# Second attention of a four-layer block: projections cut in halves over all sixteen units, GpSimd's subtractions cut in quarters

## The reference, cut to what matters

```python
h  = rmsnorm(layernorm(x)) * ln_w            # 1024 tokens x 512
q  = h @ wq.T                                # 32 heads of 16
k, v = ctx @ wk.T, ctx @ wv.T                # 8 key/value heads, 64 context rows for each batch
p  = softmax(q @ k.T / 4)                    # for each head: 256 tokens x 64 context rows
x  = x + tanh(gate) * ((p @ v) @ wo.T)
```

## Time and profile before

| what | value |
|---|---|
| time, median of 3 runs | 1511.48 us (1511.46 to 1512.91) |
| the profiled execution | 1511.66 us |
| its span | 1509.9 us |
| PE busy over the span | 1348.9 us, 89% |
| DVE busy | 1121.3 us, 74% |
| ACT, POOL busy | 677.9 us, 336.3 us |
| units of the second attention | from 475.90 us (first `turn_p`) to 576.94 us (last `weigh`) |

### The profile page before, as it was taken

One profiled execution on the slowest core, in us unless ns is written; L12 is line 12 of the kernel. 1 busy time (PEld: TensorE's weight loads), 2 busy tenths in 40 slices (PEclk: granted clock), 3 DMA queues, 4 the chain that ended last, 5 costly groups with the idle time before them and its releaser, 6 DMA issues.

```text
span 1509.9 us, 18648 instructions
## 1 busy us (share of the span) xinstructions
PE 1348.9 (89%) x6492; PEld 970.2 (64%) x6492; DVE 1121.3 (74%) x2045; ACT 677.9 (45%) x1405; POOL 336.3 (22%) x380
## 2 busy tenths in 40 slices
PE   8999999999998989967999998999999999999104
PEld 5665666566575648736888875777777777778102
DVE  4788898888898986985555576666666566567998
ACT  4778777778423434432222224443434444443104
POOL 1112121211163020332111021312222212213620
PEclk9999999999999999988999998999999999999557
DMA  5677888789710011522211210101201101000001
GB/s 218 170 180 184 221 230 209 162 211 224 213 42 1 1 56 34 107 64 50 71 42 42 96 70 1 70 28 43 70 29 43 66 14 62 1 1 1 0 0 56
DMA packets 37910, 127.74 MB, mean 85 GB/s; under 512 B 4944, under 2 KB 10960, under 8 KB 31680
## 3 DMA queue, kind: packets, MB, share of 16 engines
q1 hardware_dynamic: 26304, 83.38, 16.0%
q0 software_dynamic: 11520, 43.26, 15.0%
HBM read 72.63 MB, written 10.75 MB: 55 GB/s over the span
## 4 chain that ended last, share of the span: by engine, by line
PE 58%; DVE 23%; ACT 6%; DVEq 6%; DMA 4%; issue 2%; POOL 1%; POOLq 1%; SPq 0%
PE PS L150 12%; PE PS L152 11%; PE PS L151 11%; DVE AR L676 4%; PE PS L925 4%; PE PS L963 4%; DMA AR<-AR 2%; ACT s_sb L606 2%; DVE AR L2598 2%; PE PS L949 2%; DVE AR L2587 2%; DVE AR L2594 2%; DVEq L666 1%; DVE AR L682 1%; PE PS L1537 1%
## 5 line engine op out<-in xcount | busy, mean ns | idle before, releaser
L438 POOL DMA_DIRECT2D AR<-AR x76 | 74.9, 1104 | 339.8 <-DMA AR<-AR 125.8
L151 PE MATMUL PS<-R16r 128*128 128x512 f32 (+1 forms) x328 | 122.8, 374 | 0.0
L535 PE MATMUL PS<-R,PT 128*128 128x512 f32 x256 | 116.1, 596 | 3.7 <-DVE X L716 3.7
L152 PE MATMUL PS<-R16r 128*128 128x512 f32 (+1 forms) x312 | 119.0, 382 | 0.0
L510 PE MATMUL PS<-R,HT 128*128 128x256 f32 x512 | 116.5, 381 | 2.1 <-ACT R L595 2.1
L510 PEld LDWEIGHTS PS<-R,HT 128*128 128x128 f32 x512 | 94.8, 190 | 15.2 <-ACT R L595 3.6
L1083 ACT COPY AR<-PS 128x512 f32<-128x512 f32 x64 | 37.5, 587 | 145.9 <-PE PS L152 145.5
L606 ACT ACTIVATE s_sb<-PS,sm 128x64 f32<-128x64 f32 x256 | 78.1, 335 | 52.4 <-DVE sm L701 52.0
L150 PE MATMUL PS<-HTr,R16r 128*128 128x512 f32 (+1 forms) x240 | 91.5, 381 | 3.0 <-DVE R16r L190 1.6
L150 PE MATMUL PS<-R16r,HTr 128*128 128x512 f32 (+1 forms) x224 | 90.2, 403 | 0.0
L152 PE MATMUL PS<-HTr,R16r 128*128 128x512 f32 (+1 forms) x240 | 88.3, 368 | 0.0
(11 more groups left out here) (313 smaller groups left out, 3513.6 us busy)
## 6 DMA issues: line engine op xcount, KB each, us to landing
AR<-AR POOLq DMA_DIRECT2D x76, 528.0 KB, 6.6
OR<-in_wo SPq DMA_DIRECT2D x12, 1024.0 KB, 12.4
dequantised<-AR SPq DMA_DIRECT2D x8, 1056.0 KB, 5.5
WR<-in_w0q SPq DMA_DIRECT2D x8, 1024.0 KB, 11.4
AR<-in_w3q SPq DMA_DIRECT2D x8, 1024.0 KB, 4.9
WR<-dequantised SPq DMA_DIRECT2D x22, 256.0 KB, 2.8
AR<-in_nf SPq DMA_DIRECT2D x4, 1056.0 KB, 9.4
nf_in<-in_nf SPq DMA_DIRECT2D x4, 1056.0 KB, 10.2
```

Source lines behind the costliest of these rows:

```text
L151: nc.tensor.matmul(out, ah, bl, start=False, stop=False)
L152: return nc.tensor.matmul(out, al, bh, start=False, stop=last_)
L438: nc.gpsimd.dma_start(nf_below(g)[:, part], what[:, part], accum_op=ALU.add, max_dma_last_dim=4 * N_NF // 2).then_inc(added, 16)
L535: i = nc.tensor.matmul(bank(5 + tt), PT[:, at:at + P], vo[:, pr, b, :], start=pr == 0, stop=pr == 1)
```

## The change

`project_q` and `project_o` take a tuple of halves and issue only those matmuls; the second half counts up the semaphore. A list, `projections(u)`, says which halves follow `turn_p(u)`: one half in most units, two in units 3, 6, 8 and 14, twenty in all from unit 0 to unit 15. `add` and `dve_stats` move: `add(0,0)` and `add(0,1)` to units 8 and 9, `add(1,0)` and `add(1,1)` to 11 and 13, `add(2,0)` to 15, `add(2,1)` with its statistics behind the loop. The copies of queries on ACT move to units 1, 3, 5 and 7. Both of GpSimd's subtractions are cut into four: of the first, pieces 1, 2 and 3 wait for `probs` of 1, 2 and 3; of the second, pieces 0 to 3 wait for `probs` of 11, 12, 13 and 14. The semaphores `o_split` and `F1["split"]` count with the last piece.

```diff
@@ pool_a1
-            pool_low(Oh[:], Ol[:], OR[:]).then_inc(A1["o_split"], 1)
+            for c in range(C):
+                cols = slice(c * D, (c + 1) * D)
+                if c:
+                    pool.wait_ge(A1["probs"], c)
+                i = pool_low(Oh[:, cols], Ol[:, cols], OR[:, cols])
+            i.then_inc(A1["o_split"], 1)
@@ pe_a1
-            def project_q(b, pr):
-                if b:
+            def project_q(b, pr, halves=(0, 1)):
+                if b and halves[0] == 0:
                     pe.wait_ge(A1["qT_ready"], 2 * b - 1 + pr)
-                if b >= 3 and pr == 1:
-                    pe.wait_ge(A1["acc"], 2 * b - 4)
-                for hh in range(2):
+                for hh in halves:
...
+            def projections(u):
+                if u < 2:
+                    project_q(2, 0, (u,))
+                elif u == 2:
+                    project_q(2, 1, (0,))
+                elif u == 3:
+                    project_q(2, 1, (1,))
+                    project_q(3, 0, (0,))
+                elif u == 4:
+                    project_q(3, 0, (1,))
+                elif u == 5:
+                    project_q(3, 1, (0,))
+                elif u == 6:
+                    project_q(3, 1, (1,))
+                    project_o(0, 0, (0,))
+                elif u == 7:
+                    project_o(0, 0, (1,))
+                elif u == 8:
+                    project_o(0, 1)
+                elif u < 13:
+                    project_o(1, (u - 9) // 2, ((u - 9) % 2,))
+                elif u == 13:
+                    project_o(2, 0, (0,))
+                elif u == 14:
+                    project_o(2, 0, (1,))
+                    project_o(2, 1, (0,))
                 else:
+                    project_o(2, 1, (1,))
@@
                 turn_p(u)
-                if at < 2 and b:
-                    project_o(b - 1, at)
-                if at > 1 and b + 2 < B:
-                    project_q(b + 2, at - 2)
+                projections(u)
@@ act_a1
-                if at > 1 and b + 2 < B:
-                    queries(b + 2, at - 2)
+                if u in (1, 3, 5, 7):
+                    queries(2 + u // 4, u // 2 % 2)
@@ dve_a1
-                if 0 < hc < 3 and b:
-                    add(b - 1, hc - 1)
-                    if hc == 2:
-                        dve_stats(dve, b - 1)
+                if u == 8:
+                    add(0, 0)
+                elif u == 9:
+                    add(0, 1)
+                    dve_stats(dve, 0)
+                elif u == 11:
+                    add(1, 0)
+                elif u == 13:
+                    add(1, 1)
+                    dve_stats(dve, 1)
+                elif u == 15:
+                    add(2, 0)
             norm_low(dve, 3, 0)
             norm_scaled(dve, 3, 2)
+            add(2, 1)
             norm_low(dve, 3, 1)
             norm_scaled(dve, 3, 3)
+            dve_stats(dve, 2)
@@ pool_f1
             pool.wait_ge(F1["w_hi"], 1)
-            pool_low(Wh[:, 0:C * NWF], Wl[:, 0:C * NWF], WR[:, 0:C * NWF]).then_inc(F1["split"], 1)
+            for c in range(C):
+                cols = slice(c * NWF, (c + 1) * NWF)
+                pool.wait_ge(A1["probs"], NU - 5 + c)
+                i = pool_low(Wh[:, cols], Wl[:, cols], WR[:, cols])
+            i.then_inc(F1["split"], 1)
             pool_norm(pool, 3)
```

More of the change, by code:

```diff
@@ L1525, in project_q @@
                                 HTl[:, c, tok], c == 0, c == C - 1)
-                i.then_inc(A1["q_mm"], 1)
+                if halves[-1]:
+                    i.then_inc(A1["q_mm"], 1)
             def scores(u):
@@ L1558, in weigh, with project_o @@
                 i.then_inc(A1["pv_mm"], 1)
[L1560 to L1564, removed]
-                else:
[L1566 to L1574, removed]
+            def project_o(b, tt, halves=(0, 1)):
+                if halves[0] == 0:
+                    if tt == 0:
+                        pe.wait_ge(A1["olo"], (b + 1) * C)
+                        if b == 0:
+                            pe.wait_ge(A1["o_split"], 1)
+                    else:
+                        pe.wait_ge(A1["qT_ready"], 2 * B)
+                    if b:
+                        pe.wait_ge(A1["acc"], 2 * b - 1 + tt)
+                hi, lo = out1(b)
+                for half in halves:
+                    for hc in (2 * half, 2 * half + 1):
+                        tok = slice(hc * S + tt * P, hc * S + tt * P + P)
+                        i = mm3(bank(0 if tt else 7), hi[:, tok], lo[:, tok], Oh[:, hc * D:(hc + 1) * D],
+                                Ol[:, hc * D:(hc + 1) * D], hc == 0, hc == C - 1)
+                if halves[-1]:
+                    i.then_inc(A1["wo_mm"], 1)
```

## The result

The changed kernel takes 1514.38 us in the median of 19 runs, the kernel before 1512.21 in 19 (1509.21 to 1517.36); one run of the changed kernel was disturbed (1800.56 us) and is left out of its spread, 1511.73 to 1517.42, and of the ratio. The medians differ by 2.2 us. The ratio is 1.0018, with a 95% interval of 1.0011 to 1.0024, which is 2.7 us: slower, but just under the 0.2% that I named as the line. Forecast were +3.0 us and 1514.5.

A forecast was written before the change was run, and what follows sets the result against it. Neither PE nor DVE bounds alone: whole-projection units are PE's, units without projection DVE's. Earlier keys -0.8, longer key stretch +1.2, clock +2.5, start after landing 0.1: +3.0 on the median 1511.48 gives 1514.5 us, range 1511.6 to 1517.6.

The forecast's parts named there:

- the clock: PE after its new idling: 5 us at 1.2 GHz, half of it lost, +2.5 us.
- The turns: Turns 0 to 11, one shift to the next: 71.4 us instead of 78.3, so 6.8 us gained by turn 12.
- The quarters: GpSimd's subtractions in pieces of 1.3 and 1.8 us: 0.6 us more in all, line 360's 2.4 us block gone.
- The new wait: Last piece waits for probs 14; key weights land at 559.6, PE idles 7.6 us, first keys at 559.65.
- The second load: Query weights, 1 MB, following the key weights in SP's queue: taken as costing nothing, about 2.4 us if shared evenly.
- rival 3: Key and query weight loads share the engines: +2.4 us, 1516.9 us; chance 0.06.
- From first to last keys: Start of first keys to end of last: 19.6 us instead of 18.4, for two more halves; +1.2 us.
- Rival 1: The stall before the keys is there but the slow clock costs nothing: +0.5 us, 1512.0 us; chance 0.08.
- DVE's tail: Moved additions and statistics, about 3.1 us, lie beside PE's last keys and batch 3 outputs: covered.
- Rival 2: Longer or second slow clock stretch, as in turn 10: 2.5 us more, or 4; 1517 to 1518.5 us; chance 0.12.
- Rival 4: Key load doesn't bind, keys follow scores(15) at 552.0: last keys 7.4 us earlier, 1504.1 us; chance 0.06.
- The call on the line: Whole kernel against a 0.2% (3.0 us) line: slower 0.52, within 0.42, faster 0.06.

The follow-up runs named there:

- e7: The changed kernel plus 15 unread matmuls on PE ahead of its wait for the key weights; 1511.10 us, ratio 1.0001.
- e2: The changed kernel with both GpSimd subtractions whole again, keeping the halves and moved additions; 1503.66 us, ratio 0.9947 to the kernel before.
- e3: The kernel before with only GpSimd's subtractions cut into quarters, waiting as in the change; 1517.78 us, ratio 1.0042.
- e5: The changed kernel with each quarter of the second subtraction one probs later (12, 13, 14, 15); 1519.13 us, ratio 1.0040.
- e4: The changed kernel plus 30 unread matmuls on PE ahead of its wait for the key weights; 1516.49 us, ratio 1.0034.
- e1: The changed kernel with the second subtraction's quarters waiting in pairs, behind probs 11 and 12; 1503.59 us, ratio 0.9953 to the kernel before.
- e8: The changed kernel with the second subtraction's quarters waiting in pairs, behind probs 12 and 13; 1509.82 us, ratio 0.9985.
- e9: e1 with ScalarE copying the first two quarters of the keys ahead of its wait for unit 14's weighing; 1500.70 us, ratio 0.9927.
- e10: e2 with ScalarE's copy of the first keys moved ahead as in e9; 1501.60 us, ratio 0.9923 to the kernel before.
- e11: e1 run once more, unchanged, on the same chip as e10; 1504.40 us, ratio 0.9946 to the kernel before.

## Why the prediction was right

**The sum.** Each term can be read from the profiles. Forecast were -0.8 for the start of the first keys, +1.2 for the stretch from there to the end of the last ones, +2.5 for the clock and 0.1 for the start after landing: +3.0. Measured are -1.1 (83.3 behind turn 0 instead of 84.4), +1.4 (19.86 in e7, where the clock stayed up, less 18.4) and +2.3 (the clock): +2.6.

**The turns.** 71.4 us were forecast for turns 0 to 11, 71.40 measured; `norm(13)` ends 5.3 us into turn 12 as said. Gained over before: 554.31 - 476.04 - 71.40 = 6.9, forecast 6.8.

**The quarters.** 1.8 us each, no product blocked, and 0.1 us from release to start: right. Cutting cost GpSimd 1.1 us and not "0.6 us in all", which counted one of the two subtractions; it cost nothing on the path. But the credit that I gave them was wrong in part. I wrote that cutting makes "the 2.4 us really gone". They are gone in e2 with nothing cut, because the statistics and ScalarE's cast moved.

**The new wait.** Load issued 1.8 us behind the last piece's start, landed 4.7 us later (forecast 4.85), PE idle 7.3 us (forecast 7.6). The dose shows that the first keys follow the landing, and that the end follows them.

**The second load.** I took nothing for it. The first one landed in 4.7 us against 4.8 alone, with the second issued 0.4 us behind it: rival 3 is refuted for the changed kernel. e3, e5 and e7 have the same pair of loads and 4.8, 4.7 and 4.6 us; e4 has 6.0, which is open. The Trainium skill's rule (DMA: Bandwidth & Descriptors, Queues, rings and completion order), that a ring's descriptors are taken in order, agrees with the two rows of the changed kernel.

**From first to last keys.** 19.6 us and 2.5 for the clock were forecast, 22.1 together; 580.01 - 557.84 = 22.2 measured. Without the slow stretch it is 19.8 in e1, and e7 puts the clock at 2.3. Rival 1 (the clock costs nothing) is refuted for a wait of this length. The clock's rows were read 0.2 to 0.3 us off in the prediction: a window of 1 us at 0.82 or 0.76 splits between the two levels so that the fall before was at 547.6 and the return at 554.5, 4.0 us behind the resumed work and not 4.3. The 5 us that were taken for the slow time hold: it was 4.7 (557.84 to 562.6).

**DVE's tail.** From the end of the last keys to the transposes of the next norm it is 5.4 us before and after (585.45 - 580.01; 584.29 - 578.86): the moved additions are covered.

**The mis-sized term.** Rival 2 said that the clock may fall in turn 10 as well and cost 2.5. It does fall there in the profiles of e5, e8 and e9, and not in those of the changed kernel, e1, e2, e4, e7, e10 and e11. e1 and e11 are the same program as e9 up to there, so it differs by execution. PE's scores and DVE's next turn, in the changed kernel and then in e9:

```profile
536.86 1.98 PE L1541 MATMUL PS<-AR,R 128*128 128x512 f32 x4 [2.04 <-DVE s_sb L349]
539.81 1.21 DVE L347 TENSOR_REDUCE sm<-PS 128x16 f32<-128x1024 f32 x1
```

```profile
534.48 1.19 DVE L347 TENSOR_REDUCE sm<-PS 128x16 f32<-128x1024 f32 x1
...
537.02 3.52 PE L1541 MATMUL PS<-AR,R 128*128 128x512 f32 x4 [2.03 <-DVE s_sb L349]
540.58 1.23 DVE L347 TENSOR_REDUCE sm<-PS 128x16 f32<-128x1024 f32 x1 [0.53 <-PE PS L1541]
```

At full clock the scores end at 538.84, 1.0 us before DVE needs them. The slow ones take 1.5 us more, and turn 10 takes 6.1 us instead of 5.5 (540.58 - 534.48). So the price is 0.6: DVE bounds the turn, and I had not taken off PE's slack.

**Rival 4** (the load doesn't bind) did not come true in the change. Its price was right: 7.4 forecast for that case, 7.2 measured in e1 by the stretch, where the split lies as early as it asks.

**The call on the line.** The prediction gave 0.52 to slower by over 0.2%. The ratio, 1.0018, lies under that line, and its interval reaches over it. The mechanism and the size were right, but on which side of its own line a forecast of 3.0 us falls was luck, and the profile could not have told.

## What to carry to other kernels

A wait added to spread work out moves everything that its last piece releases: follow the semaphore at the end (here split, load, keys) to the first engine that waits for it, and compare that landing with when the user is ready; 11 us of room became 7 us of idling. Where two edits come together, run each alone: here one was worth 7 us, and the other only took them back. A stall of TensorE on the path cost its length and, on top, about 2 us at half clock, for 2.9, 7.3 and 12.9 us of idling alike in the three profiles; where DVE bounded the turn, a slow stretch cost 0.6.

## What the runs showed that I had not expected

The granted clock explains part of the spread between executions of one kernel. In the windows view, 900 to 950 us, of e1 and of e10 (window, length, PE busy, granted clock, DMA share, GB/s):

```profile
900.00:950.00 50.00, 45.53 (x221) 0.86 0.06 22
```

```profile
900.00:950.00 50.00, 44.88 (x244) 1.00 0.06 22
```

The code there is the same. Both profiles have the same wait of PE in this window:

```profile
915.55 1.97 PE L925 MATMUL PS<-OR,kvs 128*64 128x512 f32 x4 [3.06 <-DVE R16r L1217]
```

```profile
914.42 1.08 PE L925 MATMUL PS<-OR,kvs 128*64 128x512 f32 x4 [3.06 <-DVE R16r L1217]
```

In e1 the clock fell at the end of it, in the window from 915 to 916, and stayed low until 929.2, and these four matmuls took 1.97 us; in e10 it stayed up, and they took 1.08. From e10's last keys to the end of the span it is 925.0 us, where e1, e2, the changed kernel and the one before have 930.7 to 931.0. e10's five times run from 1497.37 (this profile) to 1502.84. Whether a gap of 3 us in PE's work costs the clock thus differs from one execution to the next, and a change of 0.2% needs many runs or a stage read by itself.
